# Attention operands through DRAM: each bf16 part of q and k stored once, its repeats read with a source stride of zero

## The reference, cut to what matters

```
q = (src @ Wq + bq).reshape(B, T, NHEAD, HEAD_DIM)      # 16 heads of 8 features
k = (src @ Wk + bk).reshape(B, T, NHEAD, HEAD_DIM)
scores = jnp.einsum('bqhd,bkhd->bhqk', q, k) * scale
probs = jax.nn.softmax(scores, axis=-1)
```

## Time and profile before

| | |
|---|---|
| three runs | 2153.68, 2153.75, 2157.43 us; median 2153.75 us |
| profiled execution, its own time | 2165.17 us |
| its span, first to last instruction | 2163.3 us |
| mean granted clock of TensorE | 0.957 |
| TensorE, VectorE, ScalarE, GpSimd busy | 90%, 80%, 69%, 44% of the span |
| DMA packets, bytes | 202306, 104.59 MB |
| SP's instructions per attention: stores, max loads, stack loads | 4, 16, 4 |

### The profile page before, as it was taken

The page is one execution under the profiler, slowest core; times in us unless marked ns, Lnnn a source line. Parts: engine busy times, 40 slices in busy tenths (PEclk is TensorE's granted clock), DMA queues, the critical chain, the costliest instruction groups (busy, mean ns, idle before and its releaser), DMA issues.

```text
span 2163.3 us, 48454 instructions
## 1 busy us (share of the span) xinstructions
PE 1943.5 (90%) x16928; PEld 1491.8 (69%) x16928; DVE 1724.7 (80%) x4303; ACT 1496.7 (69%) x3159; POOL 951.5 (44%) x1379
## 2 busy tenths in 40 slices
PE   4679899999999999999999999999999999986756
PEld 3566667786867777786877777786877777764534
DVE  6666887989898898988898898989898898754543
ACT  4556767878686867878686877868686867844322
POOL 5314353636444453635445463635445453433221
PEclk9889999999999999999999999999999999999777
DMA  5021222130212222120212222120212222121010
GB/s 158 7 57 12 51 55 54 47 61 21 56 39 58 53 55 56 48 60 15 63 38 58 53 55 56 45 58 19 60 43 58 53 55 54 42 56 46 5 47 6
DMA packets 202306, 104.59 MB, mean 48 GB/s; under 512 B 126664, under 2 KB 188240, under 8 KB 196944
## 3 DMA queue, kind: packets, MB, share of 16 engines
q1 hardware_dynamic: 202064, 101.48, 20.1%
HBM read 67.60 MB, written 33.55 MB: 47 GB/s over the span
## 4 chain that ended last, share of the span: by engine, by line
PE 65%; DVE 19%; POOL 5%; ACT 4%; issue 4%; SPq 1%; DMA 1%; DVEq 0%; POOLq 0%; ACTq 0%
PE psB L861 6%; PE psA L711 6%; PE psB L686 6%; DVE work L1189 5%; PE psB L849 5%; PE psA L849 4%; DVE nmax L1264 4%; PE psA L790 3%; PE psA L861 3%; PE psA L617 3%; PE psA L686 3%; PE psB L790 2%; PE psB L678 2%; PE psB L617 2%; PE psB L775 1%
## 5 line engine op out<-in xcount | busy, mean ns | idle before, releaser
L1216 DVE TENSOR_TENSOR att<-att,QK 128x1024 f32<-128x1024 f32 x192 | 271.2, 1439 | 20.1 <-ACT att L985 18.6
L1513 POOL TENSOR_TENSOR own<-X,ccoef 128x512 f32<-128x512 f32 x128 | 177.9, 1400 | 192.1 <-DVE ccoef L1208 81.4
L1189 DVE SCALAR_TENSOR_TENSOR work<-psA,c_conv_w,work 128x253 f32<-128x253 f32 (+2 forms) x495 | 222.7, 473 | 8.0 <-ACT work L943 7.0
L1264 DVE TENSOR_REDUCE nmax<-psB 128x2 f32<-128x512 f32 x288 | 189.4, 682 | 39.2 <-PE psB L752 38.8
L1400 POOL TENSOR_SCALAR var_eps<-lnmv 128x2 f32<-128x2 f32 x128 | 28.3, 221 | 389.0 <-DVE lnmv L1092 387.7
L617 PE MATMUL psA<-xnT_a,c_w_in 128*128 128x256 f32 x640 | 193.1, 401 | 6.3 <-ACT Z L968 2.2
L861 PE MATMUL psB<-c_w,hid 128*128 128x128 f32 x1408 | 192.0, 280 | 0.8 <-DVE nmax L1264 0.8
L861 PEld LDWEIGHTS psB<-c_w,hid 128*128 128x128 f32 x1408 | 177.4, 194 | 12.0 <-issue 5.6
L849 PE MATMUL psB<-x1T,c_w 128*128 128x256 f32 x544 | 164.9, 402 | 3.8 <-DVE work L1189 1.9
L1189 DVE SCALAR_TENSOR_TENSOR work<-psB,c_conv_w,work 128x255 f32<-128x255 f32 (+2 forms) x315 | 149.2, 474 | 8.1 <-ACT work L943 7.8
L1345 DVE SCALAR_TENSOR_TENSOR ff<-psB,w_e,ff 128x128 f32<-128x128 f32 x352 | 106.5, 344 | 61.4 <-PE psB L861 58.3
(11 more groups left out here) (321 smaller groups left out, 5450.9 us busy)
## 6 DMA issues: line engine op xcount, KB each, us to landing
qk_scr<-qparts SPq DMA_DIRECT2D x128, 192.0 KB, 3.0
q_stack<-qk_scr SPq DMA_DIRECT2D x96, 192.0 KB
k_stack<-qk_scr SPq DMA_DIRECT2D x32, 576.0 KB
q_max<-qk_scr SPq DMA_DIRECT2D x256, 32.0 KB, 1.9
k_max<-qk_scr SPq DMA_DIRECT2D x256, 32.0 KB, 1.8
lvl_scr<-work SPq DMA_DIRECT2D x32, 192.0 KB, 5.8
low<-lvl_scr SPq DMA_DIRECT2D x256, 1.5 KB
c_w_in<-in_in_wT SPq DMA_DIRECT2D x1, 2176.0 KB, 8.1
```

The lines of the kernel that those rows point to most:

```text
L1189: m = e.scalar_tensor_tensor(out=cv[:, back:], in0=t[:, 0:T - back], scalar=conv_w[:, c, tap:tap + 1], in1=cv[:, back:], op0=ALU.mult, op1 ...
L1216: e.tensor_tensor(att[:, :, :], att[:, :, :], bc(QK[:, kq, :], 1, HG), ALU.mult).then_inc(att_done, 1)
L1264: e.tensor_reduce(nmax[:, i, p0:p0 + 2], t[:, :].rearrange("p (h k) -> p h k", k=T), AX.X, ALU.max).then_inc(drained[b], 1)
L1513: e.tensor_tensor(own_b[k % 2][:, :].rearrange("p (h c) -> p h c", c=HD), X[:, tt, h0 * HD:(h0 + HG) * HD].rearrange("p (h c) -> p h c", c ...
```

## The change

`qk_scr` shrinks from 72 to 24 rows of 8 KB for each of q and k, so each part lies there once. k is stored by one DMA instead of three. The repeats are made when reading, by a source dimension of stride 0: for `k_max` two copies of 8 rows, for `q_stack` three copies of all 24 rows in one load, for `k_stack` three loads, one for each part, each of three copies of 8 rows. The source pattern of `q_max` is written as two times 8 rows instead of 16. The bytes that reach SBUF are the same. The counts of the semaphores follow.

```
-        qk_scrd = [nc.dram_tensor(f"qk_scr{i}", [ROW_MAX, NH, T], BF16)[:, :, :] for i in range(2)]
+        qk_scrd = [nc.dram_tensor(f"qk_scr{i}", [3 * AD, NH, T], BF16)[:, :, :] for i in range(2)]
...
                     if u:
-                        e.wait_ge(qk_stacked[k], (48, 16)[k] * u)
-
-                    if k == 0:
-                        e.dma_start(dram(qk_scrd[0], 0, [[T, P], [P * T, 3], [1, T]]), qparts[:, :, :]).then_inc(qk_stored[0], 16)
-                    else:
-                        for rep in range(3):
-                            e.dma_start(dram(qk_scrd[1], rep * P * T, [[T, P], [3 * P * T, 3], [1, T]]),
-                                        qparts[:, :, :]).then_inc(qk_stored[1], 16)
+                        e.wait_ge(qk_stacked[k], (16, 48)[k] * u)
+
+                    e.dma_start(dram(qk_scrd[k], 0, [[T, P], [P * T, 3], [1, T]]), qparts[:, :, :]).then_inc(qk_stored[k], 16)
...
-                    e.wait_ge(qk_stored[k], (16, 48)[k] * (u + 1))
+                    e.wait_ge(qk_stored[k], 16 * (u + 1))
                     for half in range(2):
                         for g in range(RG):
                             e.dma_start((q_max, k_max)[k][32 * g + 16 * half:32 * g + 16 * half + 16, :, :].rearrange("p s t -> p (s t)"),
-                                        dram(qk_scrd[k], (3 * AD * NH * T * half if k else 0) + HPG * T * g,
-                                             [[NH * T, 2 * AD], [1, HPG * T]])).then_inc(max_loaded[k], 16)
+                                        dram(qk_scrd[k], (AD * NH * T * half if k else 0) + HPG * T * g,
+                                             [[0 if k else AD * NH * T, 2], [NH * T, AD], [1, HPG * T]])).then_inc(max_loaded[k], 16)
...
                     if k == 0:
-                        for rep in range(3):
-                            e.dma_start(st[3 * AD * rep:3 * AD * (rep + 1), :, :],
-                                        dram(qk_scrd[0], 0, [[NH * T, 3 * AD], [T, NH], [1, T]])).then_inc(qk_stacked[0], 16)
+                        e.dma_start(st[0:ROW_MAX, :, :].rearrange("r s t -> r (s t)"),
+                                    dram(qk_scrd[0], 0, [[0, 3], [NH * T, 3 * AD], [1, NH * T]])).then_inc(qk_stacked[0], 16)
                     else:
-                        e.dma_start(st[0:ROW_MAX, :, :], dram(qk_scrd[1], 0, [[NH * T, ROW_MAX], [T, NH], [1, T]])).then_inc(
-                            qk_stacked[1], 16)
+                        for part in range(3):
+                            e.dma_start(st[3 * AD * part:3 * AD * (part + 1), :, :].rearrange("r s t -> r (s t)"),
+                                        dram(qk_scrd[1], part * AD * NH * T, [[0, 3], [NH * T, AD], [1, NH * T]])).then_inc(
+                                            qk_stacked[1], 16)
...
-                        e.wait_ge(qk_stacked[0], 48 * (nth[hop] + 1))
-                        e.wait_ge(qk_stacked[1], 16 * (nth[hop] + 1))
+                        e.wait_ge(qk_stacked[0], 16 * (nth[hop] + 1))
+                        e.wait_ge(qk_stacked[1], 48 * (nth[hop] + 1))
...
-                        e.wait_ge(qk_stored[1], 48 * au)
+                        e.wait_ge(qk_stored[1], 16 * au)
```

## The result

The kernel after takes **2311.09 us** (median of 4 runs, 2303.34 to 2318.62), the kernel before beside it 2155.59: a ratio of 1.0702, with a 95% interval of 1.0671 to 1.0732. That is slower, as forecast, but by 155 us where 54 were forecast, and it lies above the range's end of 2300.

A forecast was written before the change was run, and what follows sets the result against it. TensorE held 65% of the chain, with attention's DMA way mostly hidden. New idling of 28.6 (layer 1) + 2.6 + 5.5 + 6.1 + 5.7 + 5 = 53.5 us, on 2154, gave 2208 us; range 2168 to 2300.

The forecast's parts named there:

- the doubled stores' saving: Two of k's three stores removed, 384 KB per attention: `k_max` issued some 1.8 us earlier, useful only where DMAs bind.
- What was costed at nothing: Later `k_stack`, level store and level loads, POOL's wait for k's stores, and possibly dearer issuing: no time added.
- Rivals 1 and 4: 1: stacks keep 12 engines, max loads 16, 2146 us, chance 0.06; 4: way fits 14.3 us, no change, chance 0.04.
- rival 2: Only the stacks shrink to few engines, max loads stay wide: way 14.7 us, +16, 2170 us; chance 0.08.
- Rival 3: Few engines slow, 20 GB/s: 75 us in layer 1, 51 in layer 0, some 50 at ends; 2330 us; chance 0.12.
- the clock: TensorE's granted clock might lapse after new idle time: up to 1.4 us in 13 turns, 18 us.
- the length of the way: Time from the issue of q's stack load to TensorE's `smax`: 16.5 us forecast, 14.3 there in layer 1.
- the 16.5 us of the sum: Stack, k's store and `k_max` in sequence up to `smax`; in layer 1, 2.2 us of new idling, 13 times.
- hidden by 1.2 us in the forecast: Layer 0's middle attentions: the way from first `q_max` issue to `smax` takes 22.2 us against 23.4 available.
- The step: The clock allowance: up to 1.4 us per turn, from one turn's stretch taking 4.5 us instead of 3.1.
- the 5.0 us that the forecast put ahead of the stack: `q_max` loads on two engines, where the stack is issued right behind them: 21.5 us from first `q_max` issue.

## Why the prediction was wrong in its size

**Right.** Place and mechanism: the stacks on three engines, `k_max` on two; k's store ends only when the stack ahead of it is through on the first three; layer 1's `smax` stalls in 13 turns and the waits at the two ends grow; nothing of the doubled stores' saving shows. Each has its row above, and moving the load away undid it. What was costed at nothing did cost next to nothing: TensorE's waits for DMAs ahead of `es` and for the level loads came to 7.3 us, where 6.8 were. Rivals 1 and 4 fall with the shares of 0.20 and 0.12 and the 19.4 us, rival 2 with the 0.12 of `k_max`. Rival 3, slow engines at 20 GB/s, gave nearly the right total (2330), but by luck. Its rate held for `k_max` and not for the stack, as the next part shows; it had 51 us of new idling in layer 0's 13 turns, where 7 came; and it left out the clock, whose 40 us made up for much of that.

The rule cited from the Trainium skill ("DMA: Bandwidth & Descriptors") for the number of engines agrees with the shares of 0.19 and 0.12, and for `q_max` if its pattern is taken as joined (see below). Its section "Queues, rings and completion order" says that each engine consumes its descriptors in ring order; the 0.94 at 957.00, then 0.20, then 0.17 are this seen in a trace.

**The first step that failed is the length of the way**, the 16.5 us of the sum; 19.4 were measured. The measured terms are medians over layer 1's 13 turns, from the issues and from the first and last packets of each transfer in the trace:

| term | forecast | measured |
|---|---|---|
| issue of the stack load to its first data | 0.9 | 1.6 |
| the stack on three engines | 7.6 | 8.3 |
| rest of k's store behind it, landed | 1.2 | 1.1 |
| issue of `k_max` to its first data | 0.9 | 1.5 |
| data of `k_max` on two engines | 5.0 | 6.5 |
| last data to `smax` | 0.9 | 0.5 |

Two things were mis-sized. The first is the rate of an engine, taken as 26 GB/s from rows of other loads. The stack's 590 kB in 8.3 us are 24 GB/s for each of three engines, and the 262 kB of `k_max` in 6.5 us are 20 for each of two. Both terms stay within the bounds that the prediction gave them, 9.8 and 6.5 us; its middle value was too near the fast end. The second is the time before the first data. The 0.9 us hold for the kernel before, where the first packet starts 0.9 to 1.1 us after the first issue, of `k_max` as of q's stack. In the changed loads it starts 1.4 us after it or later. The time behind the last data was taken too long, 0.9 instead of 0.5 us. The 2.9 us count 13 times: 5.0 us of stall, not 2.2. In layer 0, hidden by 1.2 us in the forecast, the way is 23.9 us (1012.22 to 1036.08) and is just not hidden: 1.77 us of waiting for `k_max`, where VectorE's 1.32 stood. By the idling, the way explains 106 us, not 54.

**The second is the clock**, left out of the sum and named as up to 18 us. What the idling leaves of the 146 us is 40, and filling the waits undid 31 to 35 of them. The step took 1.4 us a turn from the earlier trace rows; the measured price is 2.8, since the lower clock came behind layer 1's wait in every turn and often behind layer 0's too.

**A smaller one**: `q_max` was expected on two engines because the 16 rows of its pattern were written in two parts. They join into one (two times 8 rows that follow each other). The windows of the last attention show it, first `q_max`, then `k_max` of after, then `q_max` of before:

```profile
2219.00:2221.00 2.00, 0.00 (x0) 0.00 (x0) 0.33 (x2) 0.00 (x0) 1.85 (x4) 1.00 0.33 82
2234.00:2238.00 4.00, 0.00 (x0) 0.00 (x0) 0.00 (x0) 0.00 (x0) 0.00 (x0) 0.50 0.11 36
```

```profile
2082.50:2084.50 2.00, 0.00 (x0) 0.00 (x0) 0.00 (x0) 0.00 (x0) 1.46 (x3) 0.63 0.33 74
```

`q_max` has 0.33 of the engines in both kernels, `k_max` 0.11. So the 5.0 us that the forecast put ahead of the stack at the ends and in layer 0 were not there (3.6 were), and that took off part of what the other terms lacked.

**Not settled**: why the changed loads begin 0.5 us or more later. It goes with the third source dimension: `k_max` with its two copies outermost (median 1.46 us after the first issue, where before had 0.95) and with 8 features outermost (1.46) alike. Why an engine carries less of `k_max`, in packets of 2 KB, than of the stack, in packets of 8 KB, was not tested either. And it is open why, of the 11.8 us of idling that the move of q's stack takes out of the kernel before, only 7 arrive in the total.

## What to carry to other kernels

Ask of a slow transfer first what stands behind it in the queue: a DMA cut for few engines holds up the shares of every later one on these engines, and the semaphore of the later one with them. Ahead of a store that somebody waits for, the same narrow load cost 140 us more than behind it; behind it, it cost at most some 10 us more than a wide one (2171.1 beside 2161.0). A saving of bytes that needs repeats in the source pattern should be priced by what the pattern's outermost count and its number of dimensions do to engines and issuing; and a stall that repeats in each turn should be priced with the lower clock behind it. And the rate of a busy engine should be taken from a row of a load of the same form, or its slow end should be in the sum.

## What the hardware showed that was not expected

- A stall of 5 us on TensorE was followed by some 6 us at the granted clock's lower level (0.50 from 974.50 to 980.50), and one of 1.7 us in layer 0 by seven (0.50 from 1165.00 to 1172.00); other waits of 1.2 to 1.9 us in layer 0 were followed by none. With the waits filled by matmuls, no lapse followed.
- An issue on SP costs by its pattern: 0.45 us for a max load of two dimensions (3.56 for 8), 0.65 with two copies outermost (5.16), 0.69 with them further in (5.52). The first data comes later too: 0.95 us after the first issue with two dimensions, 1.46 with three.
- An engine did not move 26 GB/s in every load: the eight `k_max` loads, 262 kB, took 6.5 us (median) from the first packet to the end of the last on two engines, 20 GB/s for each; the stack on three moved 24.
- Two source dimensions that join into one are taken as one: `q_max` of after took 3.57 us to issue and 0.33 of the engines, as the two-dimensional one of the kernel before did.
